# Attention value products in three fp32r passes, with the rotary and key work spread anew over the engines

## The reference

```python
q = rope(x @ Wq.T)                       # per head
k = rope(kp * kh), v = vp * vh           # one shared kp, vp; kh, vh: one factor per token and head
p = softmax(mask(q @ k.T * scale))       # causal, 512 x 512 per head
o = (p @ v) @ Wout.T
x = x + layernorm(o)                     # attention block on layernorm(x)
x = x + layernorm(moe(layernorm(x)))     # 8 experts, 2 per token, and a shared MLP
```

## Time and profile before

| | us |
|---|---|
| median of 3 runs | 801.26 |
| the runs | 799.38, 801.26, 807.01 |
| span of the profiled execution | 801.3 |
| PE, DVE, ACT, POOL busy in it | 746.7, 599.3, 500.0, 560.1 |

### The profile page before, as it was taken

How to read it: one execution, slowest core, us unless ns; L and a number is a source line. 1 busy time by engine, 2 the same in 40 slices (tenths; PEclk the granted TensorE clock), 3 DMA queues, 4 the chain that set the end, 5 groups by cost and what they waited for, 6 DMA issues and landing times.

```text
span 801.3 us, 14115 instructions
## 1 busy us (share of the span) xinstructions
PE 746.7 (93%) x4364; PEld 626.4 (78%) x4364; DVE 599.3 (75%) x1590; ACT 500.0 (62%) x1171; POOL 560.1 (70%) x465
## 2 busy tenths in 40 slices
PE   5899999999999999999989999999899988899992
PEld 4677788888888888887768888778678888898761
DVE  6658876768898877889977888998662457775675
ACT  5778777786777677666657766667523255553432
POOL 4777988888889887787869988789533534433653
PEclk9999999999999999999989999999999999999996
DMA  9312245422222221221122222112151144542332
GB/s 312 116 40 63 90 150 181 146 70 67 66 68 67 67 67 67 66 67 55 61 60 80 83 77 66 55 60 70 58 153 47 56 147 172 187 144 89 109 95 90
DMA packets 47733, 75.74 MB, mean 95 GB/s; under 512 B 9712, under 2 KB 24624, under 8 KB 47664
## 3 DMA queue, kind: packets, MB, share of 16 engines
q1 hardware_dynamic: 43504, 65.19, 25.5%
q0 software_dynamic: 3072, 8.39, 3.3%
q10 hardware_dynamic: 1088, 1.31, 0.5%
HBM read 57.71 MB, written 17.17 MB: 93 GB/s over the span
## 4 chain that ended last, share of the span: by engine, by line
PE 68%; DVE 9%; POOL 8%; issue 7%; ACT 6%; DMA 2%; DVEq 0%; another core or an unknown queue 0%; ACTq 0%; POOLq 0%
PE ps L430 19%; PE ps L976 14%; PE ps L941 13%; PE ps L992 9%; PE ps L962 7%; PE ps L1138 3%; POOL o_lo L1778 2%; POOL q_sw L1764 1%; POOL q_sw L1756 1%; POOL kh_row L1773 1%; POOL q_lo L1768 1%; POOL slot_inputs L1794 1%; ACT prob L643 1%; ACT y_sb L856 1%; DVE hid_both L1652 1%
## 5 line engine op out<-in xcount | busy, mean ns | idle before, releaser
L643 ACT ACTIVATE prob<-ps,neg_max 128x512 f32<-128x512 f32 (+3 forms) x256 | 132.5, 526 | 75.3 <-DVE neg_max L1321 75.2
L976 PE MATMUL ps<-pt,vp 128*128 128x512 f32 (+3 forms) x512 | 150.0, 436 | 8.0 <-issue 6.4
L976 PEld LDWEIGHTS ps<-pt,vp 128*128 128x128 f32 x512 | 83.0, 191 | 57.4 <-issue 26.4
L1321 DVE CUSTOM_DVE_ANT_0 ps<-ps,causal_row 128x512 f32<-128x512 f32 (+3 forms) x256 | 117.3, 520 | 0.0
L1778 POOL TENSOR_TENSOR o_lo<-o_t,o_hi 128x512 fp32r<-128x512 f32 x64 | 87.1, 1361 | 35.5 <-ACT o_hi L671 34.6
L1768 POOL TENSOR_TENSOR q_lo<-q_sw,q_hi 128x512 fp32r<-128x512 f32 x62 | 83.1, 1340 | 39.5 <-ACT q_hi L665 39.2
L962 PE MATMUL ps<-id_f,prob 128*128 128x128 f32 x640 | 92.5, 275 | 2.3 <-ACT pt L652 2.3
L941 PE MATMUL ps<-k_hi,q_hi 128*128 128x512 f32 x248 | 87.4, 352 | 3.8 <-issue 3.2
L1764 POOL TENSOR_TENSOR q_sw<-q_cos,q_sw 128x512 f32<-128x512 f32 x62 | 79.0, 1273 | 15.6 <-DVE q_cos L1313 7.4
L1334 DVE TENSOR_SCALAR pt<-ps,vcol 128x384 f32<-128x384 f32 (+2 forms) x192 | 82.3, 476 | 9.5 <-PE ps L962 9.5
L1756 POOL TENSOR_TENSOR q_sw<-q_sw,rope_sb 128x512 f32<-128x512 f32 x64 | 82.1, 1283 | 2.6 <-ACT q_sw L632 1.9
(11 more groups left out here) (219 smaller groups left out, 1946.7 us busy)
## 6 DMA issues: line engine op xcount, KB each, us to landing
kh_row<-kvh_rows SPq DMA_DIRECT2D x64, 256.0 KB, 3.1
inv_row<-inverse_sums SPq DMA_DIRECT2D x64, 256.0 KB
slot_inputs<-zeros SPq DMA_DIRECT2D x8, 640.0 KB, 4.8
xg<-slot_inputs SPq DMA_DIRECT2D x8, 640.0 KB, 4.6
slot_outputs<-yo SPq DMA_DIRECT2D x8, 640.0 KB, 3.3
up_raw<-in_w_up_dram SPq DMA_DIRECT2D x8, 368.0 KB, 4.8
wo_raw<-in_wout_dram SPq DMA_DIRECT2D x4, 512.0 KB, 7.8
dn_sb<-in_w_dn_dram SPq DMA_DIRECT2D x8, 256.0 KB, 3.7
```

What stands on the lines that cost most here:

```text
L643: ins = act.activation(prob[:, i % 2, ROW_AT[nt]:ROW_AT[nt] + w], ps_s[bank][:, at:at + w], ACT.Exp, scale=-1.0, bias=neg_max[:, i % 2, nt ...
L976: ins = pe.matmul(ps_qo[:, mt * P:SEQ], vp[:, b * TPB + mt, :], pt[:, i % 2, cols], start=(mt == 0), stop=(mt == PT_BANKS[-1][-1]))
L1321: ins = dve.tensor_tensor_reduce(s_, s_, causal_row[:, (NT - 1 - nt) * P:], 1.0, BIG, ALU.add, ALU.min, neg_max[:, i % 2, nt:nt + 1])
```

## The change

The products with tiles 0 and 1 of the probabilities (512 and 384 columns) are made in three fp32r passes, with high and low parts of the probabilities and of the values; tiles 2 and 3 stay float32. ScalarE takes tiles 0, 1 and 3 out of PSUM (`first_turned`, `second_turned`), VectorE makes the low parts of tiles 0 and 1 (`low_turned`) and takes tile 2 (`rest_turned`). High and low parts of the values are made once for each batch, by ScalarE (`head_of_values`) and GpSimd (`rest_of_values`). The probabilities and `o_lo` get single buffers. The swapped copies of queries and keys go: VectorE multiplies the halves of `ps_qo` crosswise by the sine itself (`sin_products`, `rope_products_of_keys`), from a sine table whose halves are loaded the other way round. The low part of the scaled keys moves from VectorE to GpSimd. On TensorE `turn_probs(i, [2])` moves behind the last scores, and it waits for the first low part.

```diff
-        pt = place("pt", PT_AT, [2, PACKED])
+        pt_hi = place("pt_hi", PT_AT, [SPLIT_COLS], F32R)
+        pt_rest = place("pt_rest", PT_AT + SPLIT_COLS * 4, [PACKED - SPLIT_COLS])
+        pt_lo = place("pt_lo", PT_AT + PACKED * 4, [SPLIT_COLS], F32R)
...
 ScalarE
-            def swap_q(i):
-                act.wait_ge(q_psum, i + 1)
-                if i:
-                    act.wait_ge(q_ready, i)
-                act.copy(q_sw[0:64, :], ps_qo[64:128, :])
-                act.copy(q_sw[64:128, :], ps_qo[0:64, :]).then_inc(q_swapped, 1)
...
             def first_turned(i):
                 act.wait_ge(pt_psum, 3 * i + 1)
-                if i >= 2:
-                    act.wait_ge(o_psum, i - 1)
+                if i:
+                    act.wait_ge(o_psum, i)
...
+            def second_turned(i):
+                col = batch(i) * H + head(i)
+                act.wait_ge(pt_psum, 3 * i + 2)
+                for mt in PT_BANKS[1]:
+                    bank, at = pt_slot(mt)
+                    w = SEQ - mt * P
+                    dst = turned(mt)
+                    ins = act.activation(dst, ps_pt[bank][:, at:at + w], ACT.Copy, scale=vcol[:, mt, col:col + 1])
+                ins.then_inc(pt_second_ready, 1)
...
 TensorE, turn_probs and weigh_values
                     if k == 2:
-                        pe.wait_ge(pt_first_ready, i + 1)
+                        pe.wait_ge(pt_lo_ready, 2 * i + 1)
...
-                for k, tiles in enumerate(PT_BANKS):
-                    pe.wait_ge(pt_rest_ready, 2 * i + k) if k else pe.wait_ge(pt_first_ready, i + 1)
-                    for mt in tiles:
-                        cols = slice(COL_AT[mt], COL_AT[mt] + SEQ - mt * P)
-                        ins = pe.matmul(ps_qo[:, mt * P:SEQ], vp[:, b * TPB + mt, :], pt[:, i % 2, cols],
-                                        start=(mt == 0), stop=(mt == PT_BANKS[-1][-1]))
+                pe.wait_ge(vs_ready, b + 1)
+                pe.wait_ge(pt_first_ready, i + 1)
+                pe.matmul(ps_qo[:], hi[:, 0, :], turned(0), start=True, stop=False)
+                pe.matmul(ps_qo[:], lo[:, 0, :], turned(0), start=False, stop=False)
+                pe.wait_ge(pt_second_ready, i + 1)
+                pe.matmul(ps_qo[:, P:SEQ], hi[:, 1, :], turned(1), start=False, stop=False)
+                pe.matmul(ps_qo[:, P:SEQ], lo[:, 1, :], turned(1), start=False, stop=False)
+                pe.matmul(ps_qo[:, 3 * P:SEQ], vp[:, b * TPB + 3, :], turned(3), start=False, stop=False)
+                for mt in range(SPLIT):
+                    pe.wait_ge(pt_lo_ready, 2 * i + mt + 1)
+                    pe.matmul(ps_qo[:, mt * P:SEQ], hi[:, mt, :], pt_lo[:, COL_AT[mt]:COL_AT[mt] + SEQ - mt * P],
+                              start=False, stop=False)
+                pe.wait_ge(pt_rest_ready, i + 1)
+                pe.matmul(ps_qo[:, 2 * P:SEQ], vp[:, b * TPB + 2, :], turned(2), start=False, stop=True).then_inc(o_psum, 1)
...
 TensorE, loop over the units
-                turn_probs(i, [2])
                 route_piece(i)
                 if i + 2 < UNITS:
                     scores(i + 2, [2])
+                turn_probs(i, [2])
...
 VectorE
-            def cos_q(i):
-                dve.wait_ge(q_swapped, i + 1)
+            def sin_products(i):
+                dve.wait_ge(q_psum, i + 1)
+                if i:
+                    dve.wait_ge(q_ready, i)
+                dve.tensor_tensor(q_sw[0:64, :], ps_qo[64:P, :], sin_sb[64:P, :], ALU.mult)
+                dve.tensor_tensor(q_sw[64:P, :], ps_qo[0:64, :], sin_sb[0:64, :], ALU.mult).then_inc(q_sin_ready, 1)
+
+            def cos_product(i):
                 dve.tensor_tensor(q_cos[:], ps_qo[:], cos_sb, ALU.mult).then_inc(q_cos_ready, 1)
...
+            def low_turned(i, mt):
+                if i:
+                    dve.wait_ge(o_psum, i)
+                dve.wait_ge((pt_first_ready, pt_second_ready)[mt], i + 1)
+                col = batch(i) * H + head(i)
+                bank, at = pt_slot(mt)
+                cols = slice(COL_AT[mt], COL_AT[mt] + SEQ - mt * P)
+                dve.scalar_tensor_tensor(pt_lo[:, cols], ps_pt[bank][:, at:at + SEQ - mt * P], vcol[:, mt, col:col + 1],
+                                         pt_hi[:, cols].bitcast(F32), ALU.mult, ALU.subtract).then_inc(pt_lo_ready, 1)
...
 VectorE, loop over the units
                 if i + 3 < UNITS:
-                    cos_q(i + 3)
+                    sin_products(i + 3)
+                low_turned(i, 0)
+                if i + 3 < UNITS:
+                    cos_product(i + 3)
+                low_turned(i, 1)
...
+                if i + 2 < UNITS:
+                    maxima(i + 2, [0])
                 rest_turned(i)
                 if i + 2 < UNITS:
-                    maxima(i + 2)
+                    maxima(i + 2, [1, 2])
...
                 divide_output(i)
...
-                if i + 3 < UNITS:
-                    rest_of_keys(i + 3)
...
 GpSimd, loop over the units
                     scale_keys(i + 3)
-                    sin_q(i + 3)
                     rotate(i + 3)
...
+                if i + 3 < UNITS:
+                    rest_of_keys(i + 3)
```

More of the change, by code:

```diff
@@ L155, in decoder_layer @@
         o_hi = place("o_hi", R2 + 64 * KB, [2, SEQ], F32R)
-        o_lo = place("o_lo", R2 + 68 * KB, [2, SEQ], F32R)
-        pt = place("pt", PT_AT, [2, PACKED])
+        o_lo = place("o_lo", R2 + 68 * KB, [SEQ], F32R)
+        SPLIT = 2
+        SPLIT_COLS = COL_AT[SPLIT]
+        pt_hi = place("pt_hi", PT_AT, [SPLIT_COLS], F32R)
+        pt_rest = place("pt_rest", PT_AT + SPLIT_COLS * 4, [PACKED - SPLIT_COLS])
+        pt_lo = place("pt_lo", PT_AT + PACKED * 4, [SPLIT_COLS], F32R)
+        vs_lo = [place(f"vs_lo{r}", R2 + (70 + r) * KB, [SPLIT, D], F32R) for r in range(2)]
         rope_sb = place("rope_sb", ROPE, [2 * SEQ])
@@ L260, in decoder_layer @@
         at_in, at_out = (small(n, [2, TILES], U32) for n in ("at_in", "at_out"))
+        vs_hi = [place("vs_hi0", PT_AT + (PACKED + SPLIT_COLS) * 4, [SPLIT, D], F32R), small("vs_hi1", [SPLIT, D], F32R)]
         id_in, rope_in, consts_in, w0_in = sem("id_in"), sem("rope_in"), sem("consts_in"), sem("w0_in")
@@ L345, in wo_head, with turned, values_step @@
             return i + WO_FIRST if i + WO_FIRST < H else None
+        def turned(mt):
+            at, w = COL_AT[mt], SEQ - mt * P
+            return pt_hi[:, at:at + w] if mt < SPLIT else pt_rest[:, at - SPLIT_COLS:at - SPLIT_COLS + w]
+        def values_step(b):
+            return H * b - 6
         def y_tile(b, t):
@@ L616, in values_of, with head_of_values @@
                 act.copy(vp[:, b * TPB:(b + 1) * TPB, :], ps[VALUE_BANK[b]][:]).then_inc(v_ready, 1)
+            def head_of_values(b):
+                act.wait_ge(v_ready, b + 1)
+                if b >= 2:
+                    act.wait_ge(o_psum, H * (b - 1))
+                act.copy(vs_hi[b % 2][:], vp[:, b * TPB:b * TPB + SPLIT, :]).then_inc(vs_hi_ready, 1)
             def head_of_wq(h0, h1):
@@ L768, in _ @@
                     sigmoids()
+                for b in range(1, B):
+                    if i == values_step(b):
+                        head_of_values(b)
                 if i + 3 < UNITS:
@@ L928, in scores @@
                 pe.wait_ge(q_ready, i + 1)
-                pe.wait_ge(kh_ready, i + 1)
+                pe.wait_ge(kh_ready, i + 1) if i < PLAIN else pe.wait_ge(k_lo_ready, i + 1 - PLAIN)
                 r = i % 2
@@ L986, in gather_output @@
                 pe.wait_ge(o_hi_ready, i + 1)
-                for j, (w, o_) in enumerate(((wo_hi, o_hi), (wo_lo, o_hi), (wo_hi, o_lo))):
+                for j, (w, o_) in enumerate(((wo_hi, o_hi[:, r, :]), (wo_lo, o_hi[:, r, :]), (wo_hi, o_lo[:]))):
                     if j == 2:
@@ L1492, in _ @@
             products_of_gates(0)
[L1493 removed]
+            dve.wait_ge(rope_in, 48)
             scaled_gates(0)
             sums_of_gates(0)
[L1496 removed]
+            rope_products_of_keys(0)
             rest_of(1)
[L1498 removed]
+            sin_products(0)
+            cos_product(0)
             stats_of_x(2)
             first_scaled_keys(0)
[L1501 removed]
+            rope_products_of_keys(1)
             stats_of_x(3)
@@ L1504, in _ @@
             maxima(0)
-            cos_q(1)
+            sin_products(1)
+            cos_product(1)
             first_scaled_keys(1)
             rest_of(2)
-            cos_q(2)
-            cos_of_keys(2)
+            sin_products(2)
+            cos_product(2)
+            rope_products_of_keys(2)
             inverses(0)
-            rest_of_keys(2)
             maxima(1)
@@ L1841, in _ @@
                     scatters(b, i)
+                for b in range(1, B):
+                    if i == values_step(b):
+                        rest_of_values(b)
                 if i + 3 < UNITS:
```

119 lines of the change are left out of this document (54 added, 65 removed).

## The result

| | before | after |
|---|---|---|
| median of 4 runs each, us | 800.32 | 827.07 |
| the runs, us | 799.17 to 807.01 | 825.74 to 830.01 |
| ratio, 95% interval | | 1.0314, 1.0271 to 1.0357 |
| span of the profiled execution, us | 801.3 | 823.9 |
| mean granted clock | 0.988 | 0.977 |

The change makes the kernel 3.1% slower. The profiled execution of the changed kernel took 825.74 us, so 1.8 us lie around its span. That is why the spans are only 22.6 us apart and the medians 26.7. In what follows a unit is the stretch from the division before to its own division, and units are numbered from 0, as in the code.

A forecast was written before the change was run, and what follows sets the result against it. TensorE was taken to bound plain units, VectorE the heavy ones. Terms -13.8 (TensorE), -6.1 (the 14.11 us unit), +9.4 (heavy units) and +0.8 (ends) sum to -9.7: 791.5 us, own range 784 to 797, 8 in 10 within 781 to 808.

The forecast's parts named there:

- The step that failed: 14.11 us unit: the stall at VectorE's keys' subtraction goes, -6.1 us (0 if another operation takes its place).
- last sign: Sign of being wrong: a long VectorE operation beside GpSimd stalls TensorE somewhere else; no size given.
- X: VectorE's extra work in a heavy unit: 3.94 us in the earlier trace, taken as 3.3 (2.6 to 3.9).
- TensorE, -13.8: Weighing of values in three passes: 0.23 us saved per unit, plain unit 7.74, some 60 units, -13.8 (8 to 18).
- the cover that I had called thin: Last weighing: TensorE and VectorE's third tile both there at 4.4 us; VectorE delays over 0.1 delay TensorE.
- VectorE, plain unit: VectorE's chain in a plain unit: 6.00 us, its loop 7.63, so TensorE still ends last by 0.11.
- Heavy units, +9.4: Units with extra VectorE work take 6.95 + X, four routing units 10.25 us each; +9.4 in all (0 to 14).
- ScalarE, GpSimd and the ends: ScalarE unchanged, GpSimd about 6.3 us of a 7.74 unit; before the loop and last units: +0.8 (-1 to 3).
- Rival 2: Every unit: VectorE bounds it, chain 6.64 with all overlaps lost, loop 8.27, 823 us; chance 0.1.
- Rival 3: Heavy units: TensorE's clock falls after idling, about 3 us each, four times, 803 us; chance 0.1.
- rival 1: Plain units: VectorE's chain grows to 6.2 to 6.35, units 7.83 to 7.98, 797 to 806 us; chance 0.2.
- rival 4: Heavy units cost no more than now, X being mostly waiting that goes: 782 us; chance 0.12.

The follow-up runs named there:

- the pauses: Changed kernel with five conditions that make GpSimd wait for VectorE's variance, shift, expert choice and slots: 801.45 us, 0.9985; without the last two kinds: 812.04 us, 1.0123.

## Why the prediction was wrong

Forecast 791.5, range 781 to 808; measured 827.07. The chance of 0.10 for slower was far too low.

**The step that failed** is one sentence: "No VectorE operation of the steady unit reads two large SBUF tiles any more, so that stall goes: -6.1", and with it "Part of that is waiting beside GpSimd, whose run behind the division gets one operation shorter". Small operands do not escape that wait. An addition on four numbers per partition took 2.93 us, a product of four 3.30, two products of 32 together 2.35; with the pauses they took 0.28, 0.60 and 0.38 in the mean. So unit 42 kept most of its length, units 44, 58 and 60, which I had counted as plain, became 11.4 to 11.6, and the four heavy ones went to 10.6 to 12.3 in place of 10.25. GpSimd's pauses, which take away this wait and none of the work, give 26 us back (1.0314 to 0.9985).

The prediction's bound "0 if another operation takes its place" and its last sign ("if a long VectorE operation beside GpSimd stalls TensorE somewhere else") name the case, but no rival carries it, and the price it has there is only the 6.1. In the kernel before, the keys' subtraction ahead of the addition in unit 58 took the longer wait (2.32 us at 538.15). The addition behind it shows another length of the wait (timeline of the kernel before):

```profile
539.97 1.65 POOL L1778 TENSOR_TENSOR o_lo<-o_t,o_hi 128x512 fp32r<-128x512 f32 x1
...
541.21 0.43 DVE L1381 TENSOR_SCALAR var_eps<-mv 128x4 f32<-128x4 f32 x1
...
541.58 1.29 POOL L1773 TENSOR_TENSOR kh_row<-kt,kh_row 128x512 f32<-128x512 f32 x1
```

It ended at 541.64, with the one GpSimd operation that was running (541.62), though the next followed without a gap. VectorE then still waited 1.42 us for the copied queries in the next unit, so nothing was lost. The rows that would have told it were there: the earlier trace rows has an X of 3.94 for a dozen small operations, and I took 0.6 of it for waiting, where 2.1 were (X is 1.88 with the pauses, 382.62 to 384.50).

The Trainium skill (SBUF — State Buffer, section "Who interferes with whom") says that a VectorE instruction with two SBUF inputs, or in a mode that uses two ports, and a GpSimd instruction that reads SBUF exclude each other, and that the one which starts first keeps the ports for its whole instruction. The trace agrees that the products, which have two SBUF inputs, are hit, and that the aggregates, which took 0.34 us for four beside the same run, are not; the addition has one SBUF input, and no row shows its mode. On the length the addition of the kernel before agrees; the one in unit 58 of the changed kernel differs, since its wait did not end with the GpSimd instruction that was running (554.94), but with the third in a row (557.41).

**TensorE, -13.8.** A plain unit gained 0.06, not 0.23. Of the difference 0.07 is the wait for the third tile, the cover that I had called thin: forecast were 4.4 us behind the queries for both, measured 4.4 for TensorE (251.91 to 256.29) and 4.5 for the tile (to 256.41). Another 0.06 are the two transposes right ahead of the weighing (0.28, 0.22 without passes), and the four products behind the weighing still take 0.82, so that the 0.18 which I had credited there was not to be had. The upper end of my saving, 0.35, was also added up wrongly: 2.15 belongs to 1.86, which is 0.29. The weighing itself came out a little better than I had it, 1.76 without its wait against 1.80 to 1.86; no run shows the 0.08 for changes of format by itself. In sum this costs little: of the other 51 units the 28 that stay under 8 us gave 4.0 us, where 0.23 in each would have been 6.4. The rest of the 9 us of difference, some 6.5, lies in the 23 longer ones (+8.9), most of them units with VectorE's extra work. So even with the starving gone the change is level with the kernel before (0.9985), and the passes in it cost 11 us (0.9844 without them).

**VectorE, plain unit.** 6.01 where I had 6.00. The sines and the low part behind them start 0.71, 0.72 and 0.67 after each other, where I had 0.69, 0.69 and 0.60; smaller steps behind them made up for it. Of the Trainium skill's rule on instructions in other groups of partitions (VectorE: DVE Perf Modes, "Two Vector instructions with no wait between them") I had drawn a wrong sum: it holds back the second sine half and the low part, whose full 0.69 each my 6.00 had already, and not the cosine product behind them. The trace agrees with it there: the second half starts 0.02 after the end of the first (252.82, 252.80), the low part 0.04 after the end of the second (253.54, 253.50), while the cosine product starts 0.08 before the end of the low part (254.21, 254.29). The third step is longer than I had it because the low part lasts 0.75 and not 0.68.

**Heavy units, +9.4.** The formula was good, 7.15 + X where I had 6.95 + X, since the wait for the exponentials is 0.69 (250.90) and not 0.5; X was the mistake. Units 38 and 56, in which the clock did not fall, have an X of 3.49 and 3.51 and took 10.63 and 10.66. What the stop does to the clock comes on top in the other six: in unit 58 7.15 and an X of 3.34 (554.14 to 557.48) are 10.49, and it took 11.57. By the same sum it is 0.9 to 1.5 us in each of the six, some 7 us together (an estimate).

**ScalarE, GpSimd and the ends.** No more work than forecast shows on the path; +0.9 at the ends where I had +0.8.

**The rivals.** Rival 2 had the side and by chance the time (823 with all overlaps lost), but not the mechanism: VectorE does not bound a plain unit. Rival 3, the clock in heavy units, came true in six units of the eight, with about 1.1 us in unit 58 where I had 3; it adds those 7 us to the loss and isn't its cause, since with all pauses the clock in the routing units is back at 1.00 (320 to 460 us). Plain units at 7.91 lie in rival 1's band, but the chain of 6.2 that it needed didn't come (6.01), nor did rival 4's lighter X.

Left open: why the wait lasts over three GpSimd operations in one place and over one in another. The runs show that it ends when GpSimd pauses, not what holds it.

## What to carry to other kernels

Before work is put on VectorE's chain, look at every operation ahead of it that works from SBUF to SBUF, the tiny ones too, and at what GpSimd runs beside it: its time can be that of GpSimd's whole run, though not every such operation is hit (the aggregates were not). A wait on the engine that has time to spare, so that it lets the small operation through, can be worth more than any rearranging of the busy one. And price a faster product by unit: here it pays only in units where the engine that prepares its operands has room, and that can be chosen unit by unit.

## What was not expected of the hardware

- A VectorE operation of 128x4 between SBUF tiles took 2.93 to 3.30 us beside three GpSimd operations of 1.28 to 1.31 us in a row, and 0.28 (the additions) and 0.60 (the shifts) in the mean with pauses.
- A stop of 2.14 us of TensorE was followed by 4.1 us at a granted clock of 0.58 in the mean. Of the eight stops of 2.1 to 2.7 us in the changed kernel six had the clock fall behind them (0.79 to 0.89 in the mean of the unit); those of 2.28 us in unit 38 and 2.31 in unit 56 had not, nor had the longest, 3.41 in unit 62 (granted 1.00 from 595.78 to 599.90). With the extra work behind the low part a stop of 1.58 had the clock at 0.59 behind it. So the length alone doesn't decide.
- Three conditions for GpSimd to wait, an engine with 1% of the chain that ended last, took 1.9% off the kernel, and five of them 3.2%.
